# Second phase of a sparse-attention layer: where the score products of eight slots are summed along the heads

## What is computed

```python
z = ln(x, ln1_g, ln1_b)
q, k, v = z @ Wq + bq, z @ Wk + bk, z @ Wv + bv            # (4096, 8, 64)
scores = einsum('ehd,ehd->eh', q[row], k[col]) / 8 + bias   # (131072, 8)
p = exp(scores - segment_max(scores, row)[row])
out = segment_sum(p / segment_sum(p, row)[row] * v[col], row)
x1 = x + out @ Wo + bo
y = x1 + silu(ln(x1, ln2_g, ln2_b) @ W1 + b1) @ W2 + b2
result = layernorm(x + y)
```

## Time and profile before

| | us |
|---|---|
| median of 3 runs | 3630.55 (3626.34 to 3639.14) |
| the profiled execution | 3641.99 |
| its span, first to last instruction | 3640.2 |
| busy: TensorE / VectorE / GpSimd / ScalarE | 2834.3 / 2639.6 / 2353.1 / 1731.9 |
| TensorE weight loads (beside its matmuls) | 2174.2 |
| mean granted TensorE clock | 0.866 |

### The profile page before, as it was taken

How to read it: one execution, slowest core, us unless ns; L and a number is a source line. 1 busy time by engine, 2 the same in 40 slices (tenths; PEclk the granted TensorE clock), 3 DMA queues, 4 the chain that set the end, 5 groups by cost and what they waited for, 6 DMA issues and landing times.

```text
span 3640.2 us, 82566 instructions
## 1 busy us (share of the span) xinstructions
PE 2834.3 (78%) x18693; PEld 2174.2 (60%) x18694; DVE 2639.6 (73%) x6460; ACT 1731.9 (48%) x6572; POOL 2353.1 (65%) x2550
## 2 busy tenths in 40 slices
PE   8566765666666666377888889888989898988997
PEld 6333333333333333377777777777777777777775
DVE  9677776677676667376777777777777777777774
ACT  0111111111111111276767777777777776777764
POOL 0377777777777777666666666666666666666650
PEclk9967676676766666698999999999999999999999
DMA  7222232322232322877888788788788888788780
GB/s 277 84 81 75 80 90 78 81 74 78 78 91 76 81 74 71 297 274 250 281 301 286 267 283 292 272 279 299 239 287 279 294 281 285 272 292 280 241 278 24
DMA packets 285667, 719.24 MB, mean 198 GB/s; under 512 B 86899, under 2 KB 103475, under 8 KB 285382
## 3 DMA queue, kind: packets, MB, share of 16 engines
q0 software_dynamic: 211776, 585.54, 47.3%
q1 hardware_dynamic: 73862, 133.41, 11.7%
HBM read 717.02 MB, written 72.97 MB: 217 GB/s over the span
## 4 chain that ended last, share of the span: by engine, by line
PE 36%; POOL 18%; issue 17%; DVE 8%; ACT 7%; DMA 7%; DVEq 3%; ACTq 2%; POOLq 1%; PEld 0%; SPq 0%; PEldq 0%
POOL records L410 17%; PE bank L1333 13%; ACT region_c L706 7%; PE wide L1392 6%; PE wide L1400 6%; DMA records<-region_c,pos_i 6%; PE bank L1376 3%; PE wide L1351 3%; DVE region_c L993 2%; PE bank L1232 2%; PE wide L1361 2%; POOL region_a L523 1%; ACTq L706 1%; DVE region_c L941 1%; ACTq L745 1%
## 5 line engine op out<-in xcount | busy, mean ns | idle before, releaser
L523 POOL DMA_INDIRECT region_a<-kv,cols x1160 | 1160.7, 1001 | 513.4 <-issue 456.7
L410 POOL DMA_INDIRECT records<-region_c,pos_i x1024 | 1011.5, 988 | 460.8 <-issue 293.3
L706 ACT ACTIVATE region_c<-region_a,pr 128x64 f32 x4640 | 1155.8, 337 | 44.0 <-issue 44.0
L993 DVE TENSOR_TENSOR region_c<-region_a,bank 128x1024 f32<-128x1024 f32 x580 | 671.1, 1217 | 96.2 <-issue 59.0
L1333 PE MATMUL bank<-ident,region_c 128*128 128x128 f32 x4640 | 620.4, 291 | 135.9 <-DVE region_c L993 131.7
L1333 PEld LDWEIGHTS bank<-ident,region_c 128*128 128x128 f32 x4640 | 591.1, 198 | 161.7 <-issue 151.0
L1351 PE MATMUL wide<-ident,region_c 128*128 128x128 f32 x4640 | 568.9, 276 | 77.5 <-ACT region_c L706 77.5
L1351 PEld LDWEIGHTS wide<-ident,region_c 128*128 128x128 f32 x4640 | 516.7, 144 | 111.2 <-ACT region_c L706 111.0
L628 ACT COPY region_c<-region_a 128x64 f32 x128 | 32.5, 254 | 1032.2 <-DMA records<-region_c,pos_i 1032.2
L1290 PE MATMUL bank<-region_b,region_a 128*128 128x512 f32 x768 | 496.2, 806 | 0.0
L1277 PE MATMUL wide<-region_c 64*128 64x64 f32 x2048 | 193.3, 345 | 202.1 <-issue 184.2
(11 more groups left out here) (186 smaller groups left out, 3278.2 us busy)
## 6 DMA issues: line engine op xcount, KB each, us to landing
region_a<-srcT SPq DMA_DIRECT2D x128, 256.0 KB
region_a<-kv,cols POOLq DMA_INDIRECT x1160, 5.8
region_a<-hiT SPq DMA_DIRECT2D x256, 64.0 KB
x_rows<-region_c SPq DMA_DIRECT2D x32, 512.0 KB, 3.4
records<-region_c,pos_i POOLq DMA_INDIRECT x1024
kv<-region_a SPq DMA_DIRECT2D x32, 512.0 KB
records<-region_c SPq DMA_DIRECT2D x32, 480.0 KB, 14.7
region_a<-in_x_dram SPq DMA_DIRECT2D x32, 256.0 KB, 3.2
```

The source lines that it names most:

```text
L410: pool.indirect_dma_start(records, bass.IndirectOffsetOnAxis(ap=pos_i[j % 2][:, s:s + 1], axis=0), rec_w[j % 2][:, s, :], None).then_inc(S ...
L523: pool.indirect_dma_start(KV[r][:, s, :], None, kv, bass.IndirectOffsetOnAxis(ap=cols[r][:, s:s + 1], axis=0), bounds_check=L - 1, oob_is_ ...
L706: last = act.activation(vw[:, s, of], v_part[:, s, C + hd * D:C + (hd + 1) * D], ACT.Copy, scale=pr[:, s + 1, hd:hd + 1])
L993: last = dve.tensor_tensor(prods[:, of, :], kv_in[:, of, 0:C], q_ps[:, :].unsqueeze(1).broadcast_to([P, 2, C]), ALU.mult)
```

## The change

VectorE still multiplies all eight slots. `prods_a` and `prods_b` become one signal, `prods_ready`, given after the first four slots. TensorE sums only slots 0 to 3 along the heads: 16 transposes, one matmul with `fold`. It does so in one go ahead of `turn_sum`, and `scT_ps`, `scT_sb` and `sc_ps` are half as large. In `softmax` VectorE sums slots 4 to 7 itself with one `tensor_reduce` of 32 runs of 64 numbers, drains, adds their bias, and then adds the bias of slots 0 to 3 to `sc_ps` as before. In stage 0 a drain is put behind the memset of the floor.

```diff
@@ products, VectorE
-                    if pair % 2:
-                        last.then_inc(PRODS[pair // 2], 1)
+                    if pair == 1:
+                        last.then_inc(S["prods_ready"], 1)
@@ softmax, VectorE
+                far = sc[:, SUB + 1:, :]
+                dve.tensor_reduce(far, prods[:, SUB:, :].rearrange("p s (h d) -> p s h d", h=HEADS), AX.X, ALU.add)
+                dve.drain()
+                dve.tensor_tensor(far, far, bias[:, SUB:, :], ALU.add)
                 dve.wait_ge(S["sc_summed"], groups)
-                dve.tensor_tensor(sc[:, 1:GROUP + 1, :], sc_ps.rearrange("p (s h) -> p s h", s=GROUP), bias, ALU.add)
+                dve.tensor_tensor(sc[:, 1:SUB + 1, :], sc_ps.rearrange("p (s h) -> p s h", s=SUB), bias[:, 0:SUB, :], ALU.add)
                 dve.drain()
@@ sum_d and turn_scores, TensorE
-            def sum_d(a):
-
-                if a == 0:
-                    pe.wait_ge(S["scT_sb_ready"], groups)
-                    pe.wait_ge(S["sc_ready"], groups)
-                pe.wait_ge(PRODS[a], now)
+            def sum_d():
+
+                pe.wait_ge(S["scT_sb_ready"], groups)
+                pe.wait_ge(S["sc_ready"], groups)
+                pe.wait_ge(S["prods_ready"], now)
                 for i in range(D // FOLD):
-                    last = pe.matmul(scT_ps[:, a * P:(a + 1) * P], prod_cols[:, i, a * SH:(a + 1) * SH], ident[:, :],
-                                     start=i == 0, stop=i == D // FOLD - 1, is_transpose=True)
-                if a == 1:
-                    last.then_inc(S["scT_ready"], 1)
+                    last = pe.matmul(scT_ps, prod_cols[:, i, :], ident[:, :], start=i == 0, stop=i == D // FOLD - 1, is_transpose=True)
+                last.then_inc(S["scT_ready"], 1)
 
             def turn_scores():
                 pe.wait_ge(S["scT_sb_ready"], now)
-                for a in range(2):
-                    last = pe.matmul(sc_ps[:, a * SH:(a + 1) * SH], scT_sb[:, a * P:(a + 1) * P], fold[:, :], start=True, stop=True)
-                last.then_inc(S["sc_summed"], 1)
+                pe.matmul(sc_ps, scT_sb, fold[:, :], start=True, stop=True).then_inc(S["sc_summed"], 1)
@@ body, TensorE (stage 0; the same in the others)
-                sum_d(0)
+                sum_d()
                 if stage == 0:
                     with pe.If(t > 0):
                         turn_sum()
-                    sum_d(1)
                     turn_scores()
```

More of the change, by code:

```diff
@@ L161, in layer_kernel @@
         vw = part(GROUP * C).rearrange("p (s c) -> p s c", s=GROUP)
-        scT_sb, vT_sb = part(2 * P), part(C)
+        scT_sb, vT_sb = part(P), part(C)
         assert max(used_sort, pos_c[0]) <= REGION_C
@@ L214, in layer_kernel @@
         qkv_ps = [bank[3], bank[4], bank[3]]
-        scT_ps, sc_ps = bank[0][:, 0:2 * P], bank[0][:, 2 * P:2 * P + 2 * SH]
+        scT_ps, sc_ps = bank[0][:, 0:P], bank[0][:, P:P + SH]
         vT_ps, acc_ps = bank[1], bank[7]
@@ L225, in layer_kernel @@
             qkv_done qkv_sb qkv_out place_ready placed rows_ready ng_turned ng_ready ng_out phase1_dve phase1_act
-            phase1_pe weights2 q_loaded xb_ready xb_loaded cols_ready cols_free row_ready prods_a prods_b scT_ready
+            phase1_pe weights2 q_loaded xb_ready xb_loaded cols_ready cols_free row_ready prods_ready scT_ready
             scT_sb_ready sc_summed sc_ready p_ready v_pair0 v_pair1 v_pair2 v_pair3 summed0 summed1 summed2 summed3 landed0 landed1 landed2 landed3 vT_sb_ready acc_ready acc_taken
@@ L239, in layer_kernel @@
         SUMMED = [S[f"summed{pair}"] for pair in range(PAIRS)]
-        PRODS = [S["prods_a"], S["prods_b"]]
         KVS = [[S[f"kv{h}{pair}"] for pair in range(PAIRS)] for h in range(RING)]
@@ L1322, in _ @@
                 pe.sem_inc(S[sem_of], 1)
-            prod_cols = prods.rearrange("p s (h j i) -> p i (s h) j", h=HEADS, j=FOLD)
-            def sum_d(a):
-                if a == 0:
-                    pe.wait_ge(S["scT_sb_ready"], groups)
-                    pe.wait_ge(S["sc_ready"], groups)
-                pe.wait_ge(PRODS[a], now)
+            prod_cols = prods[:, 0:SUB, :].rearrange("p s (h j i) -> p i (s h) j", h=HEADS, j=FOLD)
+            def sum_d():
+                pe.wait_ge(S["scT_sb_ready"], groups)
+                pe.wait_ge(S["sc_ready"], groups)
+                pe.wait_ge(S["prods_ready"], now)
                 for i in range(D // FOLD):
-                    last = pe.matmul(scT_ps[:, a * P:(a + 1) * P], prod_cols[:, i, a * SH:(a + 1) * SH], ident[:, :],
-                                     start=i == 0, stop=i == D // FOLD - 1, is_transpose=True)
-                if a == 1:
-                    last.then_inc(S["scT_ready"], 1)
+                    last = pe.matmul(scT_ps, prod_cols[:, i, :], ident[:, :], start=i == 0, stop=i == D // FOLD - 1, is_transpose=True)
+                last.then_inc(S["scT_ready"], 1)
             def turn_scores():
                 pe.wait_ge(S["scT_sb_ready"], now)
-                for a in range(2):
-                    last = pe.matmul(sc_ps[:, a * SH:(a + 1) * SH], scT_sb[:, a * P:(a + 1) * P], fold[:, :], start=True, stop=True)
-                last.then_inc(S["sc_summed"], 1)
+                pe.matmul(sc_ps, scT_sb, fold[:, :], start=True, stop=True).then_inc(S["sc_summed"], 1)
             def sum_v(pair):
```

## The result

| | before | changed |
|---|---|---|
| median of 4 runs, us | 3634.6 (3626.3 to 3639.1) | 3884.2 (3882.4 to 3885.8) |
| span of the profiled execution | 3640.2 | 3880.6 |
| busy: TensorE / VectorE | 2834.3 / 2639.6 | 2655.2 / 2980.1 |
| mean granted TensorE clock | 0.866 | 0.818 |

The ratio is 1.0686 (95% interval 1.0665 to 1.0708): 6.9% slower. The forecast was 3879 us.

A forecast was written before the change was run, and what follows sets the result against it. TensorE and VectorE were taken to run two rings of nearly equal length, VectorE's the longer after the change. 3642 - 117 + 2 + 363 = 3890, less 11 for the profiled execution, gives 3879 us; range 3825 to 3985.

The forecast's parts named there:

- The waits that VectorE can hide: Second phase: VectorE idle time that added work could fill, 48 (L1039) + 51 (L1012) + 18 (gathers) = 117 us.
- the register work of fourth groups: Ahead of L1039 in the 49 groups after a tile's third: 1.18 us each taken as register work, not waits.
- The price a group: New VectorE work in each of 145 groups: sum, drain and add together 2.5 us, bounds 2.1 to 3.1.
- The sum: VectorE's new sum of 2048 inputs in 32 runs of 64, once a group: 2.28 us, bounds 2.09 to 2.75.
- The add: VectorE's new 128x32 bias add, once a group: 0.19 us; with drain and smaller L1039 0.23, bounds 0.05 to 0.35.
- the 32 drains behind the memset of the floor: New VectorE drains behind L1120: 0.07 us each, 2 us in all.
- VectorE is the longer ring throughout: Second phase after the change: TensorE waits for VectorE's products in every group, so TensorE's 2.3 us relief a group doesn't count.
- The pauses on TensorE: TensorE's waits for products in the four groups of a tile: 3.7, 2.5, 4.7 and 8.1 us.
- By the tile: Check on four-group tiles: 58.1 us becomes 66.1; 8.0 us more in each of 32 is 256 us, against 248.
- Plain groups: Distance between plain groups after the change: 10.67 us plus 2.5, 13.2 us.
- Rival (1): TensorE and ScalarE ring sets the end if VectorE adds under 0.8 us a group: up to 294 us gained, 3336; chance 0.03.
- Rival (2): TensorE's clock drops in the new pauses, making it late again: 160 us more, 4040; chance of 3950 or more 0.14.

The follow-up runs named there:

- experiment 4: Kernel before with two of the four output projection matmuls (L1376) moved to the end of the tile: 3571.6 us against 3631.9, ratio 0.9836.
- experiment 1: Kernel before with VectorE's sum and drain added, all TensorE work kept: 3868.9 us against 3629.4, ratio 1.0661; on the slower occasion 4547.1 us, ratio 1.0093.
- Experiment 2: Changed kernel without VectorE's sum, slots 4 to 7 getting one product each: 3559.7 us against 3629.4 for the kernel before, ratio 0.9809.

## Why the prediction was right, by its steps

- **The waits that VectorE can hide: 117 us forecast, 134 found.** L1039 had 48 and lost 54.7 (167.2 - 112.5), L1012 had 51 and lost 59.3 (63.6 - 4.3), the gathers had 18 and lost 20.4 (36.9 - 16.5). At L1039 the step that was off is the register work of fourth groups: I gave them the 1.18 us of a fifth, and they have 1.00, as experiment 4 shows. The 1.18 us themselves are no wait: they became 1.04 in the changed kernel, as the 1.33 of third groups became 1.20 and the 0.58 of second groups, which had been called issue all along, 0.45. This 0.13 us is register work that now stands ahead of L1040. It makes 15 us, and another 15 came in at first groups (below), so the 54.7 are waits all the same. At L1012 I had left out 10 us as waits that stay, and they didn't stay.
- **The price a group: 2.5 forecast, 2.65 found.** The sum was 2.286 for 2.28, from L921 with the same run length. The add was sized right, 0.198 for 0.19. Of the 0.19 us of idle time ahead of it (27.2/145) 0.13 is the register work just named, which only changed its place, and the rest is the 0.07 of a start after a drain. What I had mis-sized is the 32 drains behind the memset of the floor: 0.07 us each forecast, 2 us in all. A first group before, in a tile without a wait, and one of the changed kernel:

```profile
3254.71 0.69 DVE L1051 SCALAR_TENSOR_TENSOR region_c<-wide,region_c 128x512 f32<-128x512 f32 x1 [0.28 <-issue]
3255.33 0.21 DVE L1039 TENSOR_TENSOR sc<-bank,region_c 128x64 f32<-128x64 f32 x1
```

```profile
3387.84 0.69 DVE L1054 SCALAR_TENSOR_TENSOR region_c<-wide,region_c 128x512 f32<-128x512 f32 x1 [0.28 <-issue]
...
3389.01 2.29 DVE L1038 TENSOR_REDUCE sc<-region_c 128x32 f32<-128x2048 f32 x1 [0.46 <-issue]
```

From start to start 0.62 us became 1.17. With the drain, the register work no longer fits beside L1051: 0.46 us of idle time stand ahead of L1038, as in second groups (0.45), where there had been none. That is some 17 us in 32 tiles. Together (sum 331, the add with its gaps some 36, drains 17) 384 us were added, where I had 365. No run has this drain alone; the 17 us are read off these rows.
- **The two errors cancel.** 384 - 134 = 250 against 240.4 between the spans (9 us not placed); the forecast had 248. That it came within 5 us of the median is luck: 19 us too little of price and 17 too little of waits.
- **VectorE is the longer ring throughout: right,** shown by experiment 1. The pauses on TensorE were 2.7, 1.2, 1.7 and 7.6 us, against 3.7, 2.5, 4.7 and 8.1. They are shorter since I had not counted that ScalarE comes late to its copy behind its own dense work (in the third group L1341 waits 2.57 us for L677), nor the slower clock (3.26 and 3.65 us for sixteen transposes, where I had 1.9).
- **By the tile:** four groups took 66.1 to 66.4 us between two loads L1111, forecast 66.1. Plain groups stand 13.1 to 13.3 us apart, forecast 13.2.
- **Rival (1)** put its turning point at 0.8 us a group. Experiment 2 adds 0.2 us and gains 70 us, so the idea of a turning point holds, but its price of up to 294 us does not: VectorE's ring alone allows only the 117 to 134 us of its waits, and gathers took some of that.
- **Rival (2)** was right in what the clock would do (0.99 to 0.90 in 3000:3500, 3.65 us for sixteen transposes after the longest pause) and wrong in what it would cost. Its step that fails is that TensorE becomes late again: VectorE waited 3.4 us in all ahead of L1011, not 51 or 160, and the rest vanished in TensorE's pauses.

## What to carry to other kernels

Before moving work from a full engine to one with a quarter of its time idle, add up that engine's idle time by releaser: only what another engine ends can take up work, and what is called issue, or stands behind a drain, can't. Of what is put down to another engine, take off the register work that would remain (here 1.33 us in each third group). The waits were 0.8 to 0.9 us a group against an added 2.5, and the busy shares (449.5 and 386.1 of 500 us) hid it. A new drain can cost more than the 0.07 us behind it, where register instructions had run beside the operation ahead of it: some 0.54 here. Where two rings are equally long, moving work within the engine from its full groups into its own pause can beat moving it to the other: here it gave 1.6% where the change lost 6.9%, and it kept the clock up as well.

## What the runs showed of the hardware

- A VectorE sum of 2048 float32 numbers into 32 took 2.286 us, one of 1024 into 16 1.220, one of 512 into 8 0.688: 1.04 ns a further input.
- Sixteen transposes took 2.04 us after pauses of 1.22 and 1.65 us and 3.26 and 3.65 us after pauses of 2.74 and 7.57. The length of the pause doesn't settle it: in the changed kernel 2.74 us were followed by 3.26 and 2.73 us by 2.05, and in the kernel before 1.82 us by 2.04 in ten tiles and by 3.50 in another one.
- What the lower clock costs depended on the slack behind it: some 1.5 us a four-group tile in the kernel before, 0.2 in the changed one.
- With a drain put behind the memset of the floor, the next operation started 1.17 us behind the start of the one ahead of the memset, and 0.62 us without it.
- The same program took 3630 us on some occasions and 4464 to 4506 on others, with equal instruction durations on VectorE and ScalarE, with TensorE idle for issue in the middle of its work, and with the untouched first phase some 400 us longer. The ratio of the same edit (experiment 1) was 1.066 on the one and 1.009 on the other, so a ratio from the one doesn't hold on the other.
